# Feed-forward of a transformer block: the hidden state is split into two 16-bit floats unnormalised, under one power of two, and the inverse root mean square multiplies the projected rows

## The reference, cut to what matters

```python
def rms_norm(x):
    eps = jnp.finfo(x.dtype).eps.astype(jnp.float32)
    xf = x.astype(jnp.float32)
    inv = jax.lax.rsqrt(jnp.mean(xf * xf, axis=-1, keepdims=True) + eps)
    return (xf * inv).astype(x.dtype)
wq_gu = ternary_quant(w_gate_up)          # levels -1, 0, 1 times a scale per group of 64
gu = jnp.einsum('bsd,hd->bsh', x, wq_gu)  # 512 -> 2 x 2048
gate, up = jnp.split(gu, 2, axis=-1)
h = jax.nn.silu(gate) * up
hn = rms_norm(h)
wq_p = ternary_quant(w_proj)
return jnp.einsum('bsh,dh->bsd', hn, wq_p)

x = L0_attn_x                             # (4, 1024, 512) float32
x = x + 0.5 * _L0_ffn_ref(_layernorm(x, axis=-1), L0_ffn_w_gate_up, L0_ffn_w_proj)
x = x + _L0_attn_ref(_layernorm(x, axis=-1), ...)
x = x + 0.5 * _L0_ffn_ref(_layernorm(x, axis=-1), L0_ffn_w_gate_up, L0_ffn_w_proj)
```

## Time and profile before

| | |
|---|---|
| median of 3 runs | 3281.08 us |
| the profiled execution | 3282.73 us, its span 3280.9 us |
| PE, share of the span | 3012.6 us, 92% |
| VectorE | 2128.2 us, 65% |
| ScalarE | 1686.4 us, 51% |
| POOL | 889.6 us, 27% |
| phase 1, first gate matmul to last projection | 184.49 to 896.50 us |
| phase 2 | 2565.61 to 3275.46 us |
| Silu L516, square L523, cast L531, per chunk | 597, 623, 618 ns |
| hidden L422, per chunk | 687 ns |
| sum of squares L566, per chunk | 1266 ns |

### The profile page before, as it was taken

One profiled execution on the slowest core, in us unless ns is written; L12 is line 12 of the kernel. 1 busy time (PEld: TensorE's weight loads), 2 busy tenths in 40 slices (PEclk: granted clock), 3 DMA queues, 4 the chain that ended last, 5 costly groups with the idle time before them and its releaser, 6 DMA issues. The chain is left out here.

```text
span 3280.9 us, 53145 instructions
## 1 busy us (share of the span) xinstructions
PE 3012.6 (92%) x16162; PEld 1150.0 (35%) x16162; DVE 2128.2 (65%) x2689; ACT 1686.4 (51%) x3156; POOL 889.6 (27%) x756
## 2 busy tenths in 40 slices
PE   1179999999999799999999999999988889999998
PEld 0134444444466322222222222222223444444444
DVE  9954333333267799999999999999922343333332
ACT  4423333333211078888888888888840233333331
POOL 6825444444344200000000000000012254444443
PEclk9999999999999789999999999999999999999999
DMA  3310111110133201111111111111237201111101
GB/s 98 110 39 0 39 38 38 38 38 26 53 94 107 70 22 30 28 28 31 31 30 30 28 30 30 28 28 28 80 103 253 68 1 39 39 38 38 38 26 39
DMA packets 163759, 160.25 MB, mean 49 GB/s; under 512 B 62552, under 2 KB 100696, under 8 KB 163680
## 3 DMA queue, kind: packets, MB, share of 16 engines
q1 hardware_dynamic: 163680, 159.23, 16.3%
HBM read 111.41 MB, written 47.19 MB: 48 GB/s over the span
## 5 line engine op out<-in xcount | busy, mean ns | idle before, releaser
L1241 DVE TENSOR_REDUCE at_neg_max<-at_max_ps 128x1 f32<-128x1024 f32 x1024 | 1205.9, 1219 | 19.8 <-PE at_max_ps L1127 0.7
L1229 ACT ACTIVATE at_probs<-at_score_ps 128x512 f32<-128x512 f32 x2048 | 1057.6, 605 | 165.0 <-PE at_score_ps L1147 165.0
L1127 PE MATMUL at_max_ps<-at_km,at_q 48*128 48x512 f16 x2048 | 705.7, 392 | 14.3 <-PEq L720 8.6
L1147 PE MATMUL at_score_ps<-at_q,at_ks 50*128 50x512 f16 x2048 | 623.9, 383 | 36.2 <-ACT at_probs L1229 19.6
L422 DVE TENSOR_TENSOR f_h<-f_gate,f_up_ps 128x512 f32<-128x512 f32 x256 | 175.7, 687 | 583.8 <-ACT f_gate L516 565.1
L1154 PE MATMUL at_out_ps<-at_probs,at_v 128*32 128x512 f32 x4096 | 546.4, 605 | 0.1
L516 ACT ACTIVATE f_gate<-f_gate_ps 128x512 f32<-128x512 f32 x256 | 152.9, 597 | 606.4 <-PE f_up_ps L604 606.4
L1423 POOL TENSOR_TENSOR rows<-rows,bias 128x512 f32<-128x512 f32 x32 | 39.4, 1264 | 1396.7 <-ACTq L1362 1312.0
L604 PE MATMUL f_gate_ps<-f_xt_hi,wt 128*128 128x512 f16 x1024 | 393.9, 385 | 21.9 <-DVE f_h L422 12.7
L566 POOL TENSOR_TENSOR f_sqsum<-f_sqsum,f_sq 128x512 f32<-128x512 f32 x224 | 283.6, 1266 | 425.5 <-ACT f_sq L523 423.6
L634 PE MATMUL f_out_ps<-wt,f_h_hi 128*128 128x512 bf16 x1024 | 390.1, 381 | 5.5 <-DVE rows L446 5.5
(11 more groups left out here) (104 smaller groups left out, 2489.8 us busy)
## 6 DMA issues: line engine op xcount, KB each, us to landing
rows<-x SPq DMA_DIRECT2D x40, 1024.0 KB, 5.7
x<-rows SPq DMA_DIRECT2D x16, 1024.0 KB, 4.4
tw_raw<-units SPq DMA_DIRECT2D x48, 256.0 KB, 2.6
at_q<-qk_parts SPq DMA_DIRECT2D x384, 32.0 KB, 1.8
rows<-x SPq DMA_DIRECT2D x32, 256.0 KB, 2.9
at_q<-at_max_parts SPq DMA_DIRECT2D x512, 1.0 KB
att<-at_out SPq DMA_DIRECT2D x256, 32.0 KB
ao_a<-att SPq DMA_DIRECT2D x8, 1024.0 KB
```

What stands on the lines that cost most here:

```text
L1127: done = nc.tensor.matmul(max_ps[u % 2][:, half * QB:(half + 1) * QB], q[k][rows, j // SLOTS, h * QB + c * P:h * QB + (c + 1) * P], km[k][ ...
L1147: nc.tensor.matmul(score_ps[pos % RING][:], ks[k][rows, kc * P:(kc + 1) * P], q[k][rows, j // SLOTS, h * QB:(h + 1) * QB], start=True, sto ...
L1229: nc.scalar.activation(probs[:, kc % PBUF, j, :], score_ps[pos % RING][:], ACT.Exp, scale=HD ** -0.5).then_inc(exps, 1)
L1241: nc.vector.tensor_reduce(neg_max[:, h, column:column + 1], max_ps[u % 2][:], AX.X, ALU.max, negate=True).then_inc(maxed, 1)
```

## The change

The hidden state isn't normalised ahead of its split. VectorE multiplies gate, up and one power of two (`hidden_range.factor`) in one instruction (L480), and the cast and the subtraction follow chunk by chunk inside the gate and up loop. `h` has 3 buffers instead of 16. The projection of tile t follows `gate_up(t)` directly, and chunk c of it waits for low part c alone. `inv` is applied as the scalar of the residual (L497), where 0.5 stood. With that `spread`, `diag` and `normalise_hidden` fall away. The mean is taken with 4/HID and 4 eps factor squared, which puts 0.5 and the factor into `inv`.

The power of two is computed once, ahead of phase 1, by `HiddenRange` from the largest weight scales, which are now kept for all 48 units (`scale`). The four turns of a tile go into four banks.

```diff
+    def pair_scales(self, dve):
+        dve.memset(self.mean_consts[:, 0:1], 4.0 / HID).then_inc(self.ready, 1)
+        dve.tensor_reduce(self.tops[:], self.scale[:, 0:2 * HC, :], AX.X, ALU.max).then_inc(self.sizing, 1)
...
+        dve.tensor_tensor(self.prods[:], tops[:, 0, :], tops[:, 1, :], ALU.mult).then_inc(self.sizing, 1)
+        dve.wait_ge(self.sizing, 2)
+        dve.tensor_reduce(self.top[:], self.prods[:], AX.X, ALU.max).then_inc(self.sizing, 1)
...
+    def find_largest(self, dve, ps):
+        dve.wait_ge(self.moved, 1)
+        dve.tensor_reduce(self.most[:], ps[0:1, 0:P], AX.X, ALU.max).then_inc(self.sizing, 1)
...
+    def make_factor(self, dve, ps):
+        dve.wait_ge(self.moved, 2)
+        dve.tensor_scalar(self.size[:], ps[:, P:P + 1], self.BOUND, None, ALU.mult).then_inc(self.sizing, 1)
...
-        turn_ps = ..., [gate_ps[1], up_ps[1]] * (DC // 2)
+        turn_ps = [gate_ps[0], up_ps[0], gate_ps[1], up_ps[1]]
...
-                nc.vector.tensor_tensor(h[:, c, :], gate[:, c % 2, :], up_ps[c % 2][:],
-                                        ALU.mult).then_inc(hs, 1)
+                if c >= HB or not first:
+                    dve.wait_ge(hlos, t * HC + (c + 1 - HB))
+                    dve.wait_ge(sqs, t * HC + (c + 1 - HB))
+                nc.vector.scalar_tensor_tensor(out=h[:, b, :], in0=up_ps[c % 2][:], scalar=hidden_range.factor,
+                                               in1=gate[:, c % 2, :], op0=ALU.mult, op1=ALU.mult).then_inc(hs, 1)
...
+            def tile(t, r):
+                gate_up(t, r, True)
+                low_parts(t + 1)
+                mean_square(t)
+                residual(t)
+
+            if balance:
+                hidden_range.pair_scales(dve)
+                hidden_range.find_largest(dve, out_ps[0])
             row_stats(0)
             dve.wait_ge(stat, SUB)
             row_moments(0)
+            if balance:
+                hidden_range.make_factor(dve, out_ps[0])
             normalise_rows(0)
...
         @block.scalar
...
                     if c >= 1:
+                        b = (r * HC + c - 1) % HB
                         act.wait_ge(hs, t * HC + c)
+                        if not first:
+                            act.wait_ge(outs, t * HC + (c - HC))
+                        nc.scalar.copy(h_hi[:, c - 1, :], h[:, b, :]).then_inc(hhis, 1)
...
-                        nc.scalar.square(sq[:, (c - 1) % 2, :], h[:, c - 1, :]).then_inc(sqs, 1)
+                        nc.scalar.square(sq[:, (c - 1) % 2, :], h[:, b, :]).then_inc(sqs, 1)
...
         @block.gpsimd
...
+            def gate_up(t, r, next_rows):
+                for c in range(HC):
+                    low_hidden(t, r, c)
+                    if c == 0:
+                        continue
...
-                    if next_rows and c == 5:
+                    if next_rows and c == 6:
                         pool.wait_ge(veps, t + 2)
                         inverse_root(rstd[:], var_eps[:], rstds)
...
         @block.tensor
...
-            def spread(t, inv_ps=inv_ps):
-                pe.wait_ge(diags, t + 1)
...
+            def tile(t):
+                gate_up(t)
+                if not (isinstance(t, int) and t == 0):
+                    pe.wait_ge(ys, t * SUB)
+                elif balance:
+                    pe.wait_ge(balance.copied, 1)
+                for c in range(HC):
+                    project(t, c)
+                    if 2 <= c < 2 + DC:
+                        turn(t + 1, c - 2)
+                    if c == 11:
+                        sum_squares(t, True)
```

More of the change, by code:

```diff
@@ L70, in steps, with ternary_weights @@
         step(k, k, True)
[L77 removed]
+def ternary_weights(nc, units, squares, square, ident16, neg_half, wt, scale, start_next):
     G = D // QG
@@ L296, in ffn @@
+def ffn(nc, name, rows, x_in, stored, src, before, dst, wt, ident, ones, neg_half, hidden_range, start_next,
+        balance=None):
     x = rows[:, 0:SUB, :]
@@ L429, in inverse_rms, with mean_square, residual @@
+            def mean_square(t):
+                dve.wait_ge(mss, t + 1)
+                nc.vector.tensor_scalar(ms[:], ms_ps[:, 0:SUB], hidden_range.mean_consts[:, 0:1],
+                                        hidden_range.mean_consts[:, 1:2], ALU.mult, ALU.add).then_inc(mean, 1)
+            def residual(t):
+                last = isinstance(t, int) and t == NTILE - 1
+                dve.wait_ge(y_in, t * 16 + 16)
                 dve.wait_ge(invs, t + 1)
                 for s in range(SUB):
-                    last = nc.vector.tensor_scalar(diag[:, s, :], ident, inv[:, s:s + 1], None, ALU.mult)
@@ L432, in inverse_rms @@
[L432 to L447, removed]
@@ L478, in _ @@
             row_moments(0)
+            if balance:
+                hidden_range.make_factor(dve, out_ps[0])
             normalise_rows(0)
             low_parts(0)
[L481 to L496, removed]
-            residual(NTILE - 2)
+            if balance:
+                dve.wait_ge(hidden_range.ready, 2)
+            tile(0, 0)
+            with dve.Fori(0, (NTILE - 2) // HB) as i:
+                for r in range(HB):
+                    tile(i * HB + (1 + r), 1 + r)
+            gate_up(NTILE - 1, NTILE - 1, False)
+            mean_square(NTILE - 1)
             residual(NTILE - 1)
@@ L623, in sum_squares @@
                 last.then_inc(mss, 1)
-            def spread(t, inv_ps=inv_ps):
-                pe.wait_ge(diags, t + 1)
-                for s in range(SUB):
-                    last = nc.tensor.matmul(inv_ps[:, s * P:(s + 1) * P], ones, diag[:, s, :],
-                                            start=True, stop=True)
-                last.then_inc(spreads, 1)
             def project_part(t, c, s):
@@ L667, in _ @@
+            if balance:
+                hidden_range.turn(pe, out_ps[0])
+                hidden_range.spread_largest(pe, out_ps[0])
             for c in range(DC):
                 turn(0, c)
-            gate_up(0)
-            gate_up(1)
-            between(1, True)
-            with pe.Fori(2, NTILE - 1) as t:
-                gate_up(t)
-                between(t, True)
-            gate_up(NTILE - 1)
-            between(NTILE - 1, False)
-            pe.wait_ge(hlos, NTILE * HC)
-            pe.wait_ge(ys, (NTILE - 1) * SUB)
+            tile(0)
@@ L679, in _ @@
+            with pe.Fori(1, NTILE - 1) as t:
+                tile(t)
+            t = NTILE - 1
+            gate_up(t)
+            pe.wait_ge(ys, t * SUB)
+            for c in range(LATE):
+                project(t, c)
+                if c == 8:
+                    sum_squares(t, False)
+            pe.wait_ge(hlos, t * HC + HC)
             for s in range(SUB):
-                for c in range(HC):
-                    last = project_part(NTILE - 1, c, s)
-                last.then_inc(outs, HC // SUB)
+                for c in range(LATE, HC):
+                    last = project_part(t, c, s)
+                last.then_inc(outs, (HC - LATE) // SUB)
@@ L1504, in macaron @@
         attended = [(semaphore, NTILE // 2 * 16) for semaphore in output_in.stored]
-        ffn(nc, "f2", rows, f_in[1], f_stored[1], x2, attended, out, wt, ident, ones, neg_half[:],
+        ffn(nc, "f2", rows, f_in[1], f_stored[1], x2, attended, out, wt, ident, ones, neg_half[:], hidden,
             lambda sp: None)
```

260 lines of the change are left out of this document (126 added, 134 removed).

## The result

| | before | changed |
|---|---|---|
| median us | 3280.37 | 3274.89 |
| lowest to highest us | 3277.47 to 3289.21 | 3265.70 to 3284.95 |
| runs of each | 20 | 20 |
| profiled execution us (span) | 3282.73 (3280.9) | 3270.28 (3268.5) |
| VectorE busy us | 2128.2 | 1996.3 |

The ratio of changed to before is 0.9981, 95% interval 0.9973 to 0.9989: 5.5 us of gain by the medians, 4 to 9 by the interval. The forecast was 3271, a gain of 10.

What follows compares the result with a forecast made beforehand. TensorE (PE), busy for the whole of a loop tile, was taken to bound the kernel. Terms -52.5 - 1.7 + 1.8 + 42 = -10.4 us gave 3271 us from 3281.1, range 3245 to 3290.

Steps and rivals of the forecast that it cites:

- What goes: PE work and halts removed from both feed-forward phases: 52.5 us less, 684.7 us per phase against 712.0 and 709.9.
- what comes: New PE stops in seven tiles of each phase, with slow clock behind them: 14 x (2.1 + 0.9) = 42 us more.
- The fourteen of the spreading: Four matmuls per tile that spread the inverse root go, 0.89 us per tile: 14 us of the 52.5.
- the 38 of halts: PE halts between tiles 0 and 1 and before the last projection, with half-clock matmuls behind them, go: 38 us.
- The start: Phase starts: four turns in four banks save 1.7 us in all; phase 1's new hidden range costs 1.8.
- The stop: PE waits at chunk 10 for hidden chunk 8 because POOL's root comes later: 2.1 us, in 14 tiles.
- The half clock: Matmuls behind each stop may run at half clock: 0.9 us taken, half the effect, ends 0 and 1.85.
- B: Rival: stop at chunk 10 small or none, 0.35 to 1.4 us without slow clock; 3234 to 3248 us; chance 0.15.
- C: Rival: POOL's operations ahead of `rstd` held up, stop at chunk 10 0.8 us longer, half clock; 3295 us; chance 0.14.
- D: Rival: projection waits for POOL part by part, the 38 us of halts stay; 3309 us; chance 0.03.

Runs made afterwards that it cites:

- range later: Changed kernel with POOL's root behind the sum of chunk 5 and all of HiddenRange moved off the start of phase 1: 3225.46 us, ratio 0.9835.
- root behind sum 5: Changed kernel with POOL's root of the next rows behind the sum of chunk 5 instead of 6, nothing else: 3226.57 us, ratio 0.9841.
- root ahead of sum 6: Changed kernel with POOL's root between the low part and the sum of chunk 6: 3254.10 us, ratio 0.9928.
- the four with stops of 1.29: Changed kernel in which POOL adds the squares of chunk 7 in one column instead of 512: 3246.38 us, ratio 0.9896.

## Why the prediction was right

The sign, the mechanism and the place held, and most sizes. The forecast gain was 10.4 us, the measured one 5.5. It is the small difference of two large sums: what goes came out some 2 us larger than forecast, what comes some 6 us larger, and the two errors partly cancel.

- **What goes (52.5).** Right. A tile without stops is 85.44 (85.47 forecast) and a phase 681.9 with its first chunk at full clock, 683.9 at half clock (684.7 forecast). The fourteen of the spreading and the 38 of halts are both shown: by the spreading put back, and by the changed kernel with the root moved, which has neither. That the first chunk runs at half clock "as now" isn't fixed: both phases of range later start at full clock.
- **The start (-1.7 and +1.8).** Right: 0.87 per phase for the banks (0.85 forecast); 1.72 in front for the range, with the other six steps beside POOL's root at no cost (L464 starts 1.68 later than before, 178.25 against 176.57). Moving the range away gave 1.70. The weights' scale with its changing address takes 1.00 us in the trace after too, as in the earlier trace rows.
- **The stop (2.1).** The mechanism was right and the size 0.3 short: a tile with the stop and without half clock is 87.85 - 85.44 = 2.41 longer. The root is 0.15 later than worked out (32.37 against 32.22), the four L464 take 3.73 instead of 3.63, and hidden chunk 8 is 0.75 us long where I kept 0.69, though the diff changes its form: 0.15 + 0.10 + 0.06. That last length also lies in the chain ahead of the root.
- **The half clock (0.9).** A guess between two rows, and it came out as one. 6 of 14 stops of the profiled execution have it, some 1.7 us each: 10 us. By the medians 3274.9 less 3226.6 less 14 x 2.41 leaves 14.6 us, 1.04 per stop, but that holds the spread of the attention too, and no trace divides it. Stops and half clock together make 44 us by the trace and 48 by the medians where 42 stood.
- **Rivals.** B (no stop) is what one moved line of POOL's order gives. C's own mechanism fell: the low part and sum ahead of `rstd` are held up by 0.15 us in all, not 0.8. Its outcome, slower than before, is what one chunk later gives, with stops of 3.79. D fell: PE never waits inside the projection.
- The Trainium skill ("SBUF — State Buffer", Who interferes with whom) lets issue order decide who is blocked for a whole instruction. By that, the first L464 at 2946.19 should be free, since POOL's low part follows at 2946.24; it takes 1.50. In the version with the root behind sum 5 POOL's started 0.12 ahead, and there too it is the first L464 that is long. But 0.05 us between a start on VectorE and one on POOL, whose times are rough, can't say who issued first, so the rule is neither borne out nor refuted. What the runs give is the price: none, one, two, three POOL operations met made the four take 1.92, 2.87, 3.81 (3.64 with the root behind sum 5) and 4.64 us, 0.8 to 1.0 for each.

What stays open is what picks the stops that are followed by the half clock. The idle time doesn't: all fourteen are 2.23 or 2.24. Open too is why the end of the attention runs at half clock for 30.72 us in two of the profiled executions and for at most 6.8 in the others.

## What to carry to other kernels

When work moves onto an engine that also feeds a small result to the critical path, look where that small result stands in the engine's order, and what the engine has ready beside the instruction that uses it: one chunk later in POOL's order (done 32.37 us into a tile instead of 28.91) cost 3.45 us, 14 times, and took away 48 of 54 us of gain. Here one chunk earlier was enough to hide both the root and the contention. And ask of every place in an order by hand whether the first tiles follow the loop's rhythm; twice here they did not.

## What the runs showed of the hardware

- TensorE's clock behind an idle stop, by granted clock and matmuls of 0.63 us: after 1.29 and 1.85 us of idle none of 28 stops in the versions that have these, after 2.24 six of 14 in one execution, after 2.29 not the only one, after 3.79 and 4.66 all sixteen. In the kernel before, one of two stops of 1.96 had it. The idle time alone doesn't order the length: some eight matmuls behind 2.24, eleven behind 4.66, and mostly thirteen behind 3.79.
- The granted clock at the end of the attention differs between executions of nearly the same program: half for 30.72 us in two profiled ones (root behind sum 5, root ahead of sum 6), for at most 6.8 in the other eight. The attention then takes 1305 us instead of 1297. So run times spread without any stop: the version with the root behind sum 5 has none, and 14 us lie between its five runs, against 19 between the changed kernel's twenty and 1.4 between the four with stops of 1.29. Whether the stops add to the spread isn't shown.
- A product of three with its scalar read per partition (L480) takes 750 ns, the product of two before it (L422) 687, on the same 128x512 tile from PSUM and SBUF.
